# Softmax attention with adaptive temperature: other positions for the next batch's preparation, and PE's helper blocks in two halves of 512 columns

## The reference, cut to what matters

```
y = (x - mean) / sqrt(var + 1e-5)             # per token
q, k, v = y @ Wq.T, y @ Wk.T, y @ Wv.T        # 16 heads of 8
l = q @ k.T / sqrt(8), causal mask
p = softmax(l); H = -sum(p * log(p + 1e-9))   # entropy of each row
poly = -0.037 H^4 + 0.481 H^3 - 2.3 H^2 + 4.917 H - 1.791
beta = where(H > 0.5, max(poly, 1), 1)
x = x + softmax(l * beta) @ v @ Wo.T + bo
```

## Time and profile before

| | |
|---|---|
| median of three runs | 2244.32 us (2239.89 to 2245.84) |
| profiled execution | 2240.57 us, span 2238.8 us |
| mean granted TensorE clock | 0.762 |
| PE busy | 1608.0 us, 72% |
| DVE busy | 1480.9 us, 66% |
| ACT busy | 1392.7 us, 62% |
| POOL busy | 140.8 us, 6% |
| softmax attention | from about 752 us to about 1957 us of the span |

### The profile page before, as it was taken

The page is one execution under the profiler, slowest core; times in us unless marked ns, Lnnn a source line. Parts: engine busy times, 40 slices in busy tenths (PEclk is TensorE's granted clock), DMA queues, the critical chain, the costliest instruction groups (busy, mean ns, idle before and its releaser), DMA issues. The chain is left out here.

```text
span 2238.8 us, 22322 instructions
## 1 busy us (share of the span) xinstructions
PE 1608.0 (72%) x6402; PEld 689.4 (31%) x6402; DVE 1480.9 (66%) x3478; ACT 1392.7 (62%) x2635; POOL 140.8 (6%) x126
## 2 busy tenths in 40 slices
PE   4787899999999643777776777767787787511166
PEld 2443344444444201222222222223222232201144
DVE  6645354535464798887787887877878773479922
ACT  4564443434333697899987999879999996300012
POOL 0000000000000100000000000000000000035364
PEclk9898899999999755676666766667666778755578
DMA  4000065454556201101011010110110102240031
GB/s 146 0 0 0 14 161 157 130 154 132 155 150 170 59 32 40 62 33 62 24 40 60 33 53 32 35 66 32 43 40 27 48 19 91 58 122 0 0 105 46
DMA packets 56667, 147.36 MB, mean 66 GB/s; under 512 B 7760, under 2 KB 22480, under 8 KB 53936
## 3 DMA queue, kind: packets, MB, share of 16 engines
q1 hardware_dynamic: 52320, 136.63, 20.1%
q0 software_dynamic: 3072, 8.39, 1.2%
q10 hardware_dynamic: 1152, 0.92, 0.3%
HBM read 126.38 MB, written 19.53 MB: 65 GB/s over the span
## 5 line engine op out<-in xcount | busy, mean ns | idle before, releaser
L1682 DVE CUSTOM_DVE_ANT_0 sa_lg<-sa_e,sa_lg 128x1024 f32<-128x1024 f32 (+7 forms) x512 | 386.7, 755 | 89.0 <-ACT sa_lg L1573 88.5
L1673 DVE CUSTOM_DVE_ANT_0 sa_e<-sa_ps,sa_mask 128x1024 f32<-128x1024 f32 (+7 forms) x512 | 385.8, 754 | 76.1 <-PE sa_ps L1423 74.5
L1563 ACT ACTIVATE sa_e<-sa_e,sa_nmax 128x1024 f32<-128x1024 f32 (+7 forms) x512 | 415.2, 811 | 29.2 <-DVE sa_nmax L1673 29.0
L1423 PE MATMUL sa_ps<-sa_space 72*128 72x512 bf16 (+3 forms) x768 | 292.4, 449 | 188.5 <-DVE sa_nmax L1673 142.9
L1573 ACT ACTIVATE sa_lg<-sa_e,sa_sum 128x1024 f32<-128x1024 f32 (+7 forms) x512 | 414.8, 810 | 4.0 <-DVE sa_prod L1682 3.6
L1581 ACT ACTIVATE sa_p<-sa_ps 128x512 f32<-128x512 f32 x576 | 346.9, 629 | 67.2 <-PE sa_ps L1475 37.7
L1472 PE MATMUL sa_ps<-sa_q2s,sa_k2s 75*128 75x512 bf16 (+3 forms) x768 | 295.0, 425 | 69.3 <-ACT sa_p L1581 57.4
L974 DVE TENSOR_TENSOR mx_hw<-mx_spread,mx_h 128x512 f32<-128x512 f32 x256 | 176.1, 691 | 232.2 <-PE mx_ps L813 192.6
L875 ACT ACTIVATE mx_h<-mx_ps 128x512 f32<-128x512 f32 (+1 forms) x264 | 157.0, 597 | 276.7 <-PE mx_ps L800 256.1
L800 PE MATMUL mx_ps<-mx_f,m 128*128 128x512 f32 x512 | 262.0, 597 | 0.8 <-ACT mx_h L875 0.8
L813 PE MATMUL mx_ps<-mx_hw,m 128*128 128x512 f32 x512 | 259.8, 594 | 0.4 <-DVE mx_hw L974 0.4
(11 more groups left out here) (322 smaller groups left out, 1864.6 us busy)
## 6 DMA issues: line engine op xcount, KB each, us to landing
mx_spread<-mx_spill SPq DMA_DIRECT2D x256, 256.0 KB, 4.0
sa_space<-sa_spill_q SPq DMA_DIRECT2D x96, 96.0 KB
sa_space<-sa_spill_k SPq DMA_DIRECT2D x96, 96.0 KB
sa_k2s<-sa_spill_k SPq DMA_DIRECT2D x48, 192.0 KB
sa_q2s<-sa_spill_q SPq DMA_DIRECT2D x48, 192.0 KB
m<-m_in SPq DMA_DIRECT2D x1, 4256.0 KB, 18.4
records<-sa_e SPq DMA_DIRECT2D x8, 512.0 KB, 5.2
be_w<-w_in SPq DMA_DIRECT2D x16, 256.0 KB, 12.1
```

The source lines that it names most:

```text
L1423: last = nc.tensor.matmul(out[:, col:col + w], q_ring[:, c % 2, local, i * P:(i + 1) * P], k_ring[:, c % 2, local, col:col + w], start=Tru ...
L1563: nc.scalar.activation(e[:, u % 5, 0:w], e[:, u % 5, 0:w], ACT.Exp, scale=-1.0, bias=nmax[:, b % 2, i, h:h + 1], accum_out=sums[:, b % 2, ...
L1673: nc.vector.tensor_tensor_reduce(out=e[:, u % 5, 0:w], in0=slot_of("unit", u)[:, 0:w], in1=mask_wide[:, SEQ - w:SEQ], scale=1.0, scalar=3. ...
L1682: nc.vector.tensor_tensor_reduce(out=lg[:, u % 2, 0:w], in0=e[:, u % 5, 0:w], in1=lg[:, u % 2, 0:w], scale=1.0, scalar=0.0, op0=ALU.mult, ...
```

## The change

No operation of the reference is computed in another way, and no buffer is added. Three things are different.

- The next batch's preparation gets a table of positions, `PREPARED`, with one DVE instruction at a position: for batch 1, made in batch 0, positions 80 to 117; for batches 2 and 3 positions 12 to 66, and 109 and 113 for v. SP's spills of q and k move with it (108 and 112; 51 and 66).
- The helper blocks a, q, k, v, wide, att and proj are made in two halves of 512 columns, each at an odd position of its own, each with its own read by DVE and its own hand-over of the slot. Beta's halves are at 5 and 7 (before: 7), att's at 13 and 15 (13), proj's at 17 and 19 (17).
- Single steps move: the split of q for the second pass to positions 8, 9, 10 and 11 (before 8, 9, 10), `copy_acc` from a group's position 4 to 3, ACT's `take_shift` behind its position's pieces, and the last batch's expert scores 2 positions later.

The other functions (`fill_a`, `fill_v`, `widen`, `turn_attended`, `out_project`, `take_a`, `take_q`, `take_v`, `take_attended`, `finish`) are cut in halves in the way that `project`, `widened` and `take_k` show. The diff, cut:

```diff
@@ -1113,7 +1113,7 @@
 GROUP_UNITS = UNITS1 // GROUPS
 AHEAD = 2
 SCORES_FROM, SCORES_STEP = ALL1 + 17, 24
-LAST_SCORES = FIRST2 + ALL1 + 18
+LAST_SCORES = FIRST2 + ALL1 + 20
 END = LAST_SCORES + SCORES_STEP
 
 
@@ -1141,10 +1141,44 @@
     return k - 1 if at == r and 1 <= k <= SIDES else None
 
 
-def batch_at(u, r):
-
-    k, at = divmod(u, UNITS1)
-    return k + 1 if at == r and k + 1 < BATCH else None
+PREPARED = (
+    {"sum": 80, "sub": 81, "square": 83, "var": 84, "root": 86, "scale": 87, "a": (91, 93), "q": (97, 99),
+     "split_q": (101, 102, 104, 105, 107), "q_out": 108, "k": (109, 111), "split_k": (112, 113, 114), "k_out": 112,
+     "v": (115, 117)},
+    {"sum": 12, "sub": 13, "square": 15, "var": 17, "root": 19, "scale": 21, "a": (25, 27), "q": (33, 37),
+     "split_q": (39, 42, 45, 48, 50), "q_out": 51, "k": (53, 57), "split_k": (59, 62, 65), "k_out": 66,
+     "v": (109, 113)})
+
+
+def step_at(u, what):
+
+    b = u // UNITS1 + 1
+    return b if b < BATCH and u % UNITS1 == PREPARED[b > 1][what] else None
+
+
+def part_at(u, what):
+
+    b = u // UNITS1 + 1
+    found = PREPARED[b > 1][what] if b < BATCH else ()
+    return (b, found.index(u % UNITS1)) if u % UNITS1 in found else (None, None)
+
+
+def half_at(u, what):
+
+    b, n = part_at(u, what)
+    return None if b is None else 2 * b + n - 1
+
+
+def batch_half(i):
+    return divmod(i + 1, 2)
+
+
+def twice(found, u, positions):
+
+    for n, r in enumerate(positions):
+        if (k := found(u, r)) is not None:
+            return 2 * k + n
+    return None
 
 
 def group_at(u, r):
...
-        WIDE_AT, SHIFT_AT = 7, 9
-        A_AT, Q_AT, K_AT, V_AT = 83, 87, 89, 107
-        TURN_AT, ATT_AT, PROJ_AT = 9, 13, 17
+        WIDE_AT, SHIFT_AT = (5, 7), 9
+        TURN_AT, BIAS_AT, ATT_AT, PROJ_AT = 9, 11, (13, 15), (17, 19)
+        half_cols = (slice(0, BANK), slice(BANK, SEQ))
+        half_tiles = (slice(0, TILES // 2), slice(TILES // 2, TILES))
 
...
-                    if (b := batch_at(u, 92)) is not None:
+                    if (b := step_at(u, "q_out")) is not None:
                         spill_first("q", b, q_split, q_parts, spill_q, q_spilled)
-                    if (b := batch_at(u, 97)) is not None:
+                    if (b := step_at(u, "k_out")) is not None:
                         spill_first("k", b, k_split, k_parts, spill_k, k_spilled)
...
-                def project(what, weights, b, done):
-                    pe.wait_ge(a_ready.sem, b + 1)
-                    out = take_slot(what, b)
-                    for n in range(HALVES):
-                        cols = slice(n * BANK, (n + 1) * BANK)
-                        last = nc.tensor.matmul(out[:, cols], mat(m3, MATS3, weights), a_cm[:, cols],
-                                                start=True, stop=True)
-                    last.then_inc(done.sem, 1)
-
...
-                def widened(k):
-                    rows, q = rows_of(k), q_cm[k // 2 % 2]
-                    dve.wait_ge(wide_mm.sem, k + 1)
-                    nc.vector.tensor_tensor(q[rows, :], slot_of("wide", k)[rows, :], q[rows, :], ALU.mult
+                def widened(i):
+                    k, n = divmod(i, 2)
+                    rows, cols, q = rows_of(k), half_cols[n], q_cm[k // 2 % 2]
+                    dve.wait_ge(wide_mm.sem, i + 1)
+                    nc.vector.tensor_tensor(q[rows, cols], slot_of("wide", i)[rows, cols], q[rows, cols], ALU.mult
                                             ).then_inc(wide_read.sem, 1)
 
                 def split_q2(k, steps):
                     rows = rows_of(k)
                     if 0 in steps:
-                        dve.wait_ge(wide_read.sem, k + 1)
+                        dve.wait_ge(wide_read.sem, 2 * (k + 1))
                         if k >= 2:
                             dve.wait_ge(q2_spilled.sem, 16 * (k - 1))
                     split_up(q_cm[k // 2 % 2][rows, :], left[rows, :], parts_of(q2_parts, rows), q2_split, steps)
 
...
-                def take_k(b):
-                    dve.wait_ge(k_mm.sem, b + 1)
-                    if b:
-                        dve.wait_ge(k_spilled.sem, 16 * b)
+                def take_a(i):
+                    b, n = batch_half(i)
+                    dve.wait_ge(a_t.sem, i + 1)
+                    nc.vector.tensor_copy(a_cm[:, half_cols[n]], slot_of("a", i)[:, half_cols[n]]).then_inc(a_ready.sem, 1)
+
+                def take_q(i):
+                    b, n = batch_half(i)
+                    dve.wait_ge(q_mm.sem, i + 1)
+                    nc.vector.tensor_scalar(q_cm[b % 2][:, half_cols[n]], slot_of("q", i)[:, half_cols[n]], -HEAD ** -0.5,
+                                            None, ALU.mult).then_inc(q_ready.sem, 1)
+
+                def take_k(i):
+                    b, n = batch_half(i)
+                    dve.wait_ge(k_mm.sem, i + 1)
+                    dve.wait_ge(k_spilled.sem, 16 * b)
                     dve.wait_ge(q_split.sem, b + 1)
-                    out, src = parts_of(k_parts), slot_of("k", b)
-                    link(nc.vector.tensor_copy(out[0], src))
-                    nc.vector.tensor_tensor(left, src, out[0], ALU.subtract).then_inc(k_read.sem, 1)
-                    dve.wait_ge(k_read.sem, b + 1)
+                    out, src = k_parts[:, 0, half_cols[n]], slot_of("k", i)[:, half_cols[n]]
+                    link(nc.vector.tensor_copy(out, src))
+                    nc.vector.tensor_tensor(left[:, half_cols[n]], src, out, ALU.subtract).then_inc(k_read.sem, 1)
+                    dve.wait_ge(k_read.sem, i + 1)
 
...
-                    if (k := side_at(u, SHIFT_AT)) is not None:
-                        take_shift(k)
...
                     for m in pieces2_at(u):
                         exp2(m)
+                    if (k := side_at(u, SHIFT_AT)) is not None:
+                        take_shift(k)
...
-                    if (k := side_at(u, WIDE_AT)) is not None:
-                        widened(k)
-                    for r in (8, 9, 10):
+                    if (i := twice(side_at, u, WIDE_AT)) is not None:
+                        widened(i)
+                    for r, steps in ((8, (0,)), (9, (1,)), (10, (2, 3)), (11, (4,))):
                         if (k := side_at(u, r)) is not None:
-                            split_q2(k, range(2 * (r - 8), min(5, 2 * (r - 8) + 2)))
-                    if (b := batch_at(u, 75)) is not None:
+                            split_q2(k, steps)
+                    if (b := step_at(u, "sum")) is not None:
                         ln.total(nc, seq(b))
-                    if (b := batch_at(u, 76)) is not None:
+                    if (b := step_at(u, "sub")) is not None:
                         ln.subtract(nc, dve, b - 1, 1, seq(b))
-                    if (b := batch_at(u, 78)) is not None:
+                    if (b := step_at(u, "var")) is not None:
                         ln.variance(nc, dve, b - 1, 1)
-                    if (b := batch_at(u, 80)) is not None:
+                    if (b := step_at(u, "scale")) is not None:
                         ln.scale(nc, dve, b - 1, 1, y_tm[:, :, :])
-                    if (b := batch_at(u, A_AT)) is not None:
-                        take_a(b)
-                    if (b := batch_at(u, Q_AT)) is not None:
-                        take_q(b)
-                        split_q(b, range(0, 3))
-                    if (b := batch_at(u, Q_AT + 1)) is not None:
-                        split_q(b, range(3, 5))
-                    if (b := batch_at(u, K_AT)) is not None:
-                        take_k(b)
-                    if (b := batch_at(u, K_AT + 1)) is not None:
-                        split_k(range(2, 4))
-                    if (b := batch_at(u, K_AT + 2)) is not None:
-                        split_k(range(4, 5))
-                    if (b := batch_at(u, V_AT)) is not None:
-                        take_v(b)
-                    if (g := group_at(u, 4)) is not None:
+                    if (i := half_at(u, "a")) is not None:
+                        take_a(i)
+                    if (i := half_at(u, "q")) is not None:
+                        take_q(i)
+                    b, step = part_at(u, "split_q")
+                    if b is not None:
+                        split_q(b, (step,))
+                    if (i := half_at(u, "k")) is not None:
+                        take_k(i)
+                    b, step = part_at(u, "split_k")
+                    if b is not None:
+                        split_k((2 + step,))
+                    if (i := half_at(u, "v")) is not None:
+                        take_v(i)
+                    if (g := group_at(u, 3)) is not None:
                         copy_acc(g)
                     if (g := group_at(u, TURN_AT)) is not None:
                         normalise(g)
-                    if (b := done_at(u, ATT_AT - 2)) is not None:
+                    if (b := done_at(u, BIAS_AT)) is not None:
                         add_bias(b)
```

(52 more changed lines are left out.)

85 lines of the change are left out of this document (44 added, 41 removed).

## The result

The changed kernel takes 2228.88 us (median of 7, 2223.09 to 2234.06), the kernel before, run beside it, 2244.32 (median of 7, 2239.89 to 2247.15): ratio 0.9933, interval 0.9917 to 0.9949. It is faster by 15 us, where 47 were forecast. The profiled execution has a span of 2226.7 us (before 2238.8) at a mean granted clock of 0.753 (0.762). Busy times barely moved: PE 1622.6, DVE 1482.7, ACT 1396.0 us.

A forecast was written before the change was run, and what follows sets the result against it. ACT bounds the calm heads; elsewhere dense helper work makes it wait for PE and DVE. Terms 29.8 + 7.2 + 2.4 + 10 - 2.5 = 47 us off 2240.6 give 2194, median 2197; own case 2178 to 2215, range 2168 to 2228.

The forecast's parts named there:

- So a half costs 0 to 0.9; I take 0.3, nearer to the free one: Preparation's halved blocks: each half costs 0.3 us on the path, 2.4 for eight (bounds 0 and 7.2).
- the att and proj term: Att and proj in halves, batches 1 to 3: 0.8 of 2.5 us gained, three times, 2.4 in all.
- preparation, batches 1 and 2: Spreading the next batch's preparation regains 14.9 of 19.6 us in each batch: 29.8 (bounds 20 and 35).
- side ends, six: Beta's block in halves at 5 and 7 gains 1.2 us per side's end, 7.2 for six in batches 1 to 3.
- batch 0, from position 64: Preparation moved later in batch 0: 3.5 us gained, then 6.5, together 10 (bounds 3 and 18).
- tail: After unit 511, where nothing covers, second wide half, `copy_acc` and halved att and proj lose 2.5 us (bounds 0 and 5).
- the turned block that costs 0 in calm heads: Evidence for cheap halves: a group's whole turned block costs ACT nothing in calm heads.
- v at 0.9: Evidence for a half's price: a batch 0 head, calm but for whole block v, took 16.6 us, 0.9 above 15.68.
- PE at the low clock: Rival: if PE's clock falls to 0.5, PE bounds and 12 us of each preparation return: 2222; chance 0.13.
- more work goes with more clock: Argument against the low-clock rival: denser stretches show a granted clock of 0.69 to 0.79, calm ones 0.64.
- The norm's part: Batch 0, positions 64 to 86: norm's scale and copy of a leave, side's end improves; 3.5 us gained.
- hand-overs: Rival: each passing of the wide slot costs 2.8 us, so more halves lose: 2313; chance 0.08, no gain from 1.6.

The follow-up runs named there:

- e13: The changed kernel with all its helper blocks whole again and beta's whole block at position 5: 2206.80 us, ratio 0.9828 to the kernel before.
- e7: The changed kernel with its helper blocks whole, and each group's turned block cut in two halves (positions 9 and 11): ratio 0.9914 to the kernel before.
- e5: The changed kernel with its helper blocks whole, each of the 28 made twice on PE without added hand-overs: ratio 1.0003 to the kernel before.
- e2: The changed kernel with only att and proj whole again (positions 13 and 17): ratio 0.9898 to the kernel before.
- e9: The changed kernel with each matmul of the second pass's pieces made twice on PE: ratio 0.9961 to the kernel before.
- e10: The changed kernel with its helper blocks whole and each matmul of the second pass's pieces made twice on PE: ratio 0.9933 to the kernel before.
- e6: The changed kernel with the scores of each narrow unit made twice on PE: ratio 0.9913 to the kernel before.

## Why the prediction was wrong

The mechanism of the gain was right, and with whole blocks the sum nearly holds. What failed is the step "So a half costs 0 to 0.9; I take 0.3, nearer to the free one": measured, it is 0.8 for each more hand-over, with what the clock adds to it. The one beside it, that beta's halves at 5 and 7 bring each side's end 1.2 us, failed too, and the att and proj term had the wrong sign. By its terms, in us gained, each from the profiled executions (the preparation's cost is a stretch of batch 1 or 2 less the same of batch 3; side ends and att and proj are three times batch 3's):

| term | forecast | the change | e13 |
|---|---|---|---|
| preparation, batches 1 and 2 | 29.8 | 21.2 | 28.3 |
| side ends, six | 7.2 | -1.5 | 5.8 |
| att and proj, three | 2.4 | -7.8 | -6.3 |
| batch 0, from position 64 | 10 | 5.8 | 9.1 |
| tail | -2.5 | -7.1 | -1.5 |
| the rest | 0 | 1.5 | -1.0 |
| sum | 47 | 12.1 | 34.4 |

*Preparation.* Forecast 4.7 us left of 19.6 in each batch. In e13 5.4 are left in batch 2 (39.1 - 38.3, 98.0 - 94.1, 37.3 - 36.1, and 35.5 - 36.1), so DVE's slack covers the spread work as it was worked out. In the change 9.6 are left (1.3, 4.2, 2.1, 2.0): the halves cost 4.2 us more for four more hand-overs, about 1 each; in batch 1 it is 2.9 (8.1 left for 5.2), 0.7 each. I had 2.4 for all eight halves. The 28 extra hand-overs of the change (12 of a, q, k and v, 8 of wide, 4 each of att and proj) are together the 22.3 us between the two spans, 0.8 each: near the upper bound, where I took a value near the lower. Of the two rows I leaned on, the turned block that costs 0 in calm heads did not carry: in e7 its second half costs 0.45 there. The other, v at 0.9, stood at a clock of 0.81, and the change runs these heads at 0.64. And PE's own work for a block counts: in e5 1.05 us of each block reaches the time. DVE's busy time rose by 1.8 us, where I had some 5, so DVE's own work isn't what made the halves dear.

*Side ends.* The early place was worth what I said (e13: 2.0 us at positions 64 to 80, none at the sides where a batch starts), but only to a whole block. I had followed the halves, and left out that the wide unit between them comes late.

*Att and proj.* Forecast +0.8 each, measured -2.6. Of that the halves are only 0.4 in batch 3 (36.5 to 36.1 in e13). Most of the rest is the clock. The second half projection of batch 3 and its read, in the change:

```profile
1765.04 2.05 PE L1556 MATMUL sa_ps<-m,sa_attc 128*128 128x128 f32 x8 [0.64 <-DVE sa_nmax L1712]
...
1767.13 0.69 DVE L1843 TENSOR_TENSOR x_res<-sa_ps,x_res 128x512 f32<-128x512 f32 x1
```

The whole one, in the kernel before:

```profile
1780.98 2.02 PE L1517 MATMUL sa_ps<-m,sa_attc 128*128 128x128 f32 x16 [1.01 <-DVE sa_nmax L1673]
```

And the whole one in e13:

```profile
1742.93 3.76 PE L1568 MATMUL sa_ps<-m,sa_attc 128*128 128x128 f32 x16 [0.89 <-DVE sa_nmax L1724]
```

Eight records in the change take as long as sixteen before: this stretch had a granted clock of 0.79 before, mostly 2.4 GHz, and has 0.64 now (0.63 in e13), mostly 1.2. The 1.74 us between 2.02 and 3.76 is most of what e13 loses there. In the kernel before, the projections of batches 1 and 2 already took 3.76 us, and their stretches 37.2 and 37.3. Batch by batch the change loses 1.3, 1.2 and 2.6 there, 5.1 in all; by three times batch 3 the table has 7.8, with the rest in the preparation's favour. Why the clock fell in a stretch whose work is the same stays open. Over the three batches of all kernels the stretch took between 33.2 us (at 0.86) and 38.6 (at 0.60); with a whole projection, 33.2 to 35.2 where that took 2.0 us, and 35.3 to 37.3 where it took 3.3 to 3.8. The Trainium skill ("TensorE: Matmul & The Clock Gate", the section on a second failure mode, PSUM-queue depth-cycling) tells of a kernel in which the clock goes back and forth between its two levels, since PE idles for short times between groups of matmuls. The trace agrees that both levels occur within one such stretch (0.64 on the mean, PE busy 29.0 of 36.5 us); that the idles bring the change of level no run here shows. So the rival "PE at the low clock" (2222, the nearest figure) had a true part, but not its own: it had 12 us come back in each preparation, where e13 holds what was forecast. My sentence against it, "more work goes with more clock", does not hold from one kernel to the next: in the six heads from position 64 PE went from 87.3 of 122.9 us at 0.69 to 84.0 of 110.2 at 0.64.

*Tail.* Forecast -2.5, of it 0.65 for the second wide half. The last side's end in the change (SPq is SP's queue):

```profile
1815.64 1.97 PE L1468 MATMUL sa_ps<-m,sa_bwide 128*64 128x128 f32 x8 [2.75 <-DVE sa_bwide L1745]
...
1818.19 1.09 ACT L1620 ACTIVATE sa_p<-sa_ps 128x512 f32<-128x512 f32 x2 [3.96 <-PE sa_ps L1509]
...
1820.88 1.37 PE L1468 MATMUL sa_ps<-m,sa_bwide 128*64 128x128 f32 x8
1822.28 0.69 DVE L1760 TENSOR_TENSOR sa_q<-sa_ps,sa_q 64x512 f32<-64x512 f32 x1 [3.94 <-PE sa_ps L1468]
...
1827.69 0.63 SPq L1379 DMA_DIRECT2D sa_spill_q<-sa_q2p  x1
```

in e2, which has beta's block in the same halves:

```profile
1809.10 1.09 PE L1480 MATMUL sa_ps<-m,sa_bwide 128*64 128x128 f32 x8 [1.93 <-DVE sa_bwide L1757]
...
1811.95 1.09 PE L1480 MATMUL sa_ps<-m,sa_bwide 128*64 128x128 f32 x8
...
1818.49 0.63 SPq L1389 DMA_DIRECT2D sa_spill_q<-sa_q2p  x1
```

and in e13:

```profile
1798.29 1.96 PE L1480 MATMUL sa_ps<-m,sa_bwide 128*64 128x128 f32 x16 [2.53 <-DVE sa_bwide L1757]
...
1806.24 0.63 SPq L1389 DMA_DIRECT2D sa_spill_q<-sa_q2p  x1
```

The second half is not waiting for the first one's read; it is behind pieces and an answer in PE's queue, 3.3 us after the first half's end. The spill that the next group hangs on leaves 12.05 us after the block was begun, in e13 7.95. That is 4.1 of the 5.6 us between the tails of the change and e13. Only a part of it is the halves': in e2, where the clock stayed at 1.00, the spill leaves after 9.39 us, 1.4 later than with the whole block. The other 2.7 are the clock's, which was 0.50 from 1816 to 1820 us in the change, so that its first eight records took as long as sixteen in e13. The remaining 1.5 us of the 5.6 lie at the end, where att and proj in halves had 0.7 in my sum: from the last piece's exp to the last expert scores it is 34.1 us in the change and 32.5 in e13.

*Batch 0.* The norm's part held (5.0 us gained from 64 to 86, forecast 3.5). From 86 to 128 it was 0.9 for 6.5; with whole blocks and the early wide 3.2. So here my figure for the spread preparation was too high whatever the blocks, and why is open.

The rival *hand-overs* was right in kind and too dear in size: 0.8 us each, not 2.8, below the 1.6 from which it decides (it counted 25 more of them, without the three behind unit 511). A low price, 28 times, took more than half of what the positions bring. How much of the 0.8 is the hand-over itself and how much the lower clock that the halves met is not separated for the program as a whole: e9 against e10 leaves about half of the loss at the high clock, and the tail 1.4 of 4.1 us.

## What to carry to other kernels

Spreading dense helper work over positions where the engine that makes it has slack returns what the count of busy time promises. Cutting a helper block in halves is another matter: where the blocks share one buffer with the main work and an engine takes its list in order, more hand-overs can cost (here 0.45 us each in calm places, 0.8 on the mean, and 1.9 in the tail, 5.6 us for three, with the clock's part in them; eight in the kernel before cost nothing that could be measured), so try to move the whole block earlier before cutting it. Two edits of one change should be priced apart: here the positions alone, with beta's block whole and two positions earlier, bring 1.72% (ratio 0.9828), and the halves took 1.05 points of that away.

## What the runs showed of the hardware

The granted clock of a stretch changed with no work of that stretch changed: att and proj of batch 3, the same work, lay at 0.79 in the kernel before and 0.63 in e13; and in e6, within one execution, at 0.64 in batch 1 and 0.80 in batch 2, with 37.9 and 33.4 us. At 1.2 GHz a projection in sixteen records takes 3.76 us, at 2.4 GHz 2.02, so that one block alone can account for 1.7 us of such a stretch. More matmuls for PE can lift the clock (0.85 in batch 3 of e9, with 2.3 us less in that stretch), but not always (e6 stayed at 0.64 there), and cost more elsewhere: the tail of e9 is 153.1 us against the change's 149.3. Two kernels should be compared by the clock of each stretch before a difference of some 2 us is read as the edit's.
